# Two causal attentions: the order of score blocks, value products and turned outputs taken from a table per layer, and the row maxima of a wide row chained from its first half

## The reference, cut to what matters

```python
# layer 0: 16 heads of 8 features; layer 1: 16 heads of 64 features, keys and values made from 32 shared features
scores = jnp.einsum('bhqd,bhkd->bhqk', q, k) * scale        # B, H, S, S = 4, 16, 1024, 1024
scores = jnp.where(causal, -jnp.inf, scores)                # a query sees the keys up to its own place
attn = jax.nn.softmax(scores, axis=-1)
out = jnp.einsum('bhqk,bhkd->bhqd', attn, v)
```

## Time and profile before

| | us |
|---|---|
| median of 3 runs (2075.58 to 2084.6) | 2078.56 |
| the profiled execution | 2072.83 |
| its span | 2071.1 |
| PE busy (share of span) | 1879.1 (91%) |
| DVE busy | 1435.9 (69%) |
| ACT busy | 1193.8 (58%) |
| stretch 120 to 584, thirteen and more loaded steps of the first attention: PE, DVE busy of 464 | 450.35, 370.00 |
| stretch 1050 to 1674, thirty steps of the second attention: PE, DVE busy of 624 | 623.60, 418.01 |

### The profile page before, as it was taken

The page is one execution under the profiler, slowest core; times in us unless marked ns, Lnnn a source line. Parts: engine busy times, 40 slices in busy tenths (PEclk is TensorE's granted clock), DMA queues, the critical chain, the costliest instruction groups (busy, mean ns, idle before and its releaser), DMA issues. The chain is left out here.

```text
span 2071.1 us, 39995 instructions
## 1 busy us (share of the span) xinstructions
PE 1879.1 (91%) x9924; PEld 1169.6 (56%) x9926; DVE 1435.9 (69%) x6257; ACT 1193.8 (58%) x2252; POOL 622.0 (30%) x955
## 2 busy tenths in 40 slices
PE   5799999999986729994899999999999999899998
PEld 3455555555536527872445555555555558678886
DVE  6788777777826827875766666666666636887776
ACT  5266666666664728981445555555555558555554
POOL 4011111111120774762011111111111110567665
PEclk9799999999995869996989999999999999999999
DMA  6423233433305112224946464655555512546562
GB/s 214 123 35 64 42 61 44 61 48 55 49 8 207 36 56 70 75 76 132 362 112 145 104 139 106 136 111 130 116 126 122 119 35 81 138 93 131 128 121 61
DMA packets 107198, 210.87 MB, mean 102 GB/s; under 512 B 16540, under 2 KB 46378, under 8 KB 105680
## 3 DMA queue, kind: packets, MB, share of 16 engines
q1 hardware_dynamic: 99840, 194.98, 40.8%
q0 software_dynamic: 4992, 8.48, 1.3%
q10 hardware_dynamic: 2256, 6.21, 1.0%
HBM read 163.01 MB, written 47.89 MB: 102 GB/s over the span
## 5 line engine op out<-in xcount | busy, mean ns | idle before, releaser
L679 DVE CUSTOM_DVE_ANT_0 a1ms<-a1S,mask_q 128x128 bf16<-128x128 f32 (+1 forms) x758 | 387.9, 553 | 173.5 <-issue 170.6
L736 ACT ACTIVATE a1work<-a1T 128x512 f32<-128x512 f32 x576 | 330.2, 597 | 297.4 <-PE a1T L838 296.9
L679 DVE CUSTOM_DVE_ANT_0 a0ms<-a0S,mask_q 128x384 bf16<-128x384 f32 (+2 forms) x752 | 379.7, 553 | 97.5 <-issue 90.4
L736 ACT ACTIVATE a0work<-a0T 128x512 f32<-128x512 f32 x576 | 330.0, 597 | 186.6 <-PE a0T L838 175.7
L817 PE MATMUL a1O<-a1work,a1v 128*33 128x512 f32 (+3 forms) x1536 | 304.6, 496 | 0.9 <-POOL a1work L647 0.9
L838 PE MATMUL a0T<-a0qT,a0kT 128*128 128x512 f32 (+3 forms) x768 | 265.3, 392 | 15.9 <-ACT a0work L736 5.1
L838 PE MATMUL a1T<-a1qT,a1kT 97*128 97x512 f32 (+3 forms) x768 | 263.3, 391 | 2.0 <-DMA a1qT<-a1mr 2.0
L838 PEld LDWEIGHTS a1T<-a1qT,a1kT 97*128 97x128 f32 x768 | 131.6, 189 | 202.0 <-ACT a1work L736 144.5
L777 PE MATMUL a0S<-a0kS,a0qS 128*128 128x384 f32 (+2 forms) x752 | 229.9, 362 | 17.2 <-PEq L305 9.1
L1997 POOL TENSOR_TENSOR attn<-attn 128x512 f32<-128x512 f32 x136 | 201.4, 1496 | 105.8 <-DVE attn L1899 104.7
L838 PEld LDWEIGHTS a0T<-a0qT,a0kT 128*128 128x128 f32 x768 | 131.4, 189 | 170.2 <-ACT a0work L736 126.5
(11 more groups left out here) (336 smaller groups left out, 3333.2 us busy)
## 6 DMA issues: line engine op xcount, KB each, us to landing
attn<-scr_g SPq DMA_DIRECT2D x32, 1024.0 KB, 9.8
a1qT<-scr_q SPq DMA_DIRECT2D x93, 256.0 KB, 4.1
a1qS<-scr_q SPq DMA_DIRECT2D x90, 256.0 KB, 6.3
a1kT<-scr_k SPq DMA_DIRECT2D x93, 128.0 KB, 4.8
a1kS<-scr_k SPq DMA_DIRECT2D x90, 128.0 KB, 7.0
scr_q<-p_own SPq DMA_DIRECT2D x16, 512.0 KB, 5.1
scr_q<-attn SPq DMA_DIRECT2D x16, 512.0 KB, 7.4
scr_slots<-wp SPq DMA_DIRECT2D x1, 5980.0 KB, 18.2
```

The costliest lines, as they stand in the source:

```text
L679: nc.vector.tensor_tensor_reduce(masked_s[spare][:, 0:c1 - c0], buf[:, 0:c1 - c0], k.mask_q[:, SEQ - w + c0:SEQ - w + c1], 1.0, NEVER, ALU ...
L736: nc.scalar.activation(prob_of(g, p)[:, h, :], t_ps[slot % 2][:, :], ACT.Exp, scale=scale)\
```

## The change

A class `Order` holds, for each layer, the order of the 12 units of a head (`blocks`, now single halves), the place of the turned maxima in it (`mark`), the slot of every unit (`units`), of every value product (`values`, numbers past the last slot fall into the next step), and of the two turned output halves (`outs`). Units of one slot may now be many, and slots may have none. The lead has 6 units (before four items, also 6 units). In layer 0 the first lead unit stands in slot 31 (before 33) and the last value product in slot 2 of the next step (before 3). In layer 1 the first lead unit stands in slot 12 (before 15) and the last two value products in slot 2 of the next step (before 17 and 1), with the first product of the new step right behind them. L686 is gone: the second half of a wide row starts its maximum from the first half's result (`floor`), and waits on DVE until that is there.

```diff
+ORDER_0 = Order(((6, 0), (3, 0), (4, 0), (7, 0), (2, 0), (0, 0), (1, 0), (6, 1), (5, 0), (7, 1), (5, 1), (4, 1)),
+                5,
...
+                (9, 13, 17, 21, 25, 27, 30, 35, 38), (4, 7))
+ORDER_1 = Order(((1, 0), (4, 0), (5, 0), (6, 0), (6, 1), (4, 1), (5, 1), (2, 0), (7, 0), (7, 1), (3, 0), (0, 0)),
+                3,
+                (0, 0, 0, 0, 1, 3, 3, 3, 3, 4, 5, 6, 8, 9, 9, 10, 10, 10, 11, 12, 12, 13, 13, 15, 16, 16),
+                (2, 8, 8, 11, 11, 14, 16, 20, 20), (5, 6))
...
-    LEAD = 4
-    BLOCKS = [b for i in reversed(range(TPB // 2)) for b in (TPB // 2 + i, i)]
-    PBUF = 3 * BURST if BURST == 1 else 2 * BURST
+    LEAD, PBUF = 6, 3
...
-            NRED += 3 if i == BLOCKS[-1] and HALVES == 2 else 2
+            NRED += 2
             MAXIMA[h, i, half] = NRED
+    HEAD_DONE = [max(n for (head, _, _), n in MAXIMA.items() if head == h) for h in range(HG)]
...
+    ahead_units = [(*x, a, slot) for (x, a), slot in zip([(x, 1) for x in chain[LEAD:]] + [(x, 2) for x in chain[:LEAD]], order.units)]
+    out_units = [("o", 0, 0, half, -1, slot) for half, slot in enumerate(order.outs)]
...
     VALUES, CARRIED = ({s: [] for s in range(NSLOT)} for _ in range(2))
-    for p in range(NP):
-        for part in range(PARTS):
-            s = (p // BURST * BURST + BURST) * HG - 1 + DELAY + part * (HG // PARTS)
-            (VALUES[s] if s < NSLOT else CARRIED[s - NSLOT]).append((p, part))
+    for p, s in enumerate(order.values):
+        (VALUES[s] if s < NSLOT else CARRIED[s - NSLOT]).append(p)
...
-    COPY_0 = next(s for s in VALUES if (LAST_OF_BANK[0], PARTS - 1) in VALUES[s]) + 1
-    COPY_1 = max(s for s in CARRIED if CARRIED[s]) + 1
-    OUT_AT = COPY_1 + 2
+    COPY_AT = [order.values[p] + 1 for p in LAST_OF_BANK]
...
+                            if half:
+
+                                dve.wait_ge(red_done, lin(gU, NRED, MAXIMA[h, i, 0]))
                             dve.wait_ge(unit_ready, base + (n + 1))
                             nc.vector.memset(held[:, spare:spare + 1], 0.0).then_inc(red_done, 1)
 
                             found = mhalf[par][:, h, i - TPB // 2:i - TPB // 2 + 1] if wide and half == 0 else mmax[par][:, h, i:i + 1]
+                            floor = NEVER
+                            if half:
+                                floor = mhalf[par][:, h, i - TPB // 2:i - TPB // 2 + 1]
                             nc.vector.tensor_tensor_reduce(masked_s[spare][:, 0:c1 - c0], buf[:, 0:c1 - c0],
-                                                           k.mask_q[:, SEQ - w + c0:SEQ - w + c1], 1.0, NEVER,
+                                                           k.mask_q[:, SEQ - w + c0:SEQ - w + c1], 1.0, floor,
                                                            ALU.add, ALU.max, found).then_inc(red_done, 1)
-                            if i == BLOCKS[-1] and HALVES == 2:
-
-                                dve.wait_ge(red_done, lin(gU, NRED, MAXIMA[h, i, half] - 1))
-                                upper = mmax[par][:, h, TPB // 2:TPB]
-                                nc.vector.tensor_tensor(upper, upper, mhalf[par][:, h, :], ALU.max).then_inc(red_done, 1)
...
-                        if (h, i, half) == (0, BLOCKS[0], 0):
+                        if (kind, h, i, half) == chain[0]:
 
                             pe.wait_ge(ldS[gU[1]], gU[0] * (16 * NLOAD) + 16 * NLOAD)
...
-                        pe.wait_ge(red_done, lin(gU, NRED, MAXIMA[h, BLOCKS[-1], 0]))
+                        pe.wait_ge(red_done, lin(gU, NRED, HEAD_DONE[h]))
```

More of the change, by code:

```diff
@@ L463, in attention @@
     NLOAD = operands.NLOAD
[L464 to L467 removed]
+    LEAD, PBUF = 6, 3
+    assert 2 * NP % PBUF == 0
     DIAGONALS = [[(off, seg) for off, seg in zip((0, p[0][2] - p[0][1]), p) if seg[1] == seg[0] * P] for p in PIECES]
@@ L477, in attention @@
     for h in range(HG):
[L478 to L486, removed]
+        blocks = [("S", h, *x) for x in order.blocks]
+        chain += blocks[:order.mark] + ([("m", h - 1, 0, 0)] if h else []) + blocks[order.mark:]
+    chain.append(("m", HG - 1, 0, 0))
     MAXIMA, NRED = {}, 0
-    for kind, h, i, half, _, _ in units_from([(*x, 0) for x in chain]):
+    for kind, h, i, half in chain:
         if kind == "S":
-            NRED += 3 if i == BLOCKS[-1] and HALVES == 2 else 2
+            NRED += 2
             MAXIMA[h, i, half] = NRED
[L495 to L498, removed]
+    HEAD_DONE = [max(n for (head, _, _), n in MAXIMA.items() if head == h) for h in range(HG)]
+    start_units = [(*x, 0, 0) for x in chain] + [(*x, 1, 0) for x in chain[:LEAD]]
+    NLEAD, NU = LEAD, len(chain)
     START_MAXIMA = NRED + MAXIMA[start_units[-1][1:4]]
@@ L585, in before @@
                 return [last_of[bank] for bank in main_ring(unit_slot(g))]
-            units = units_from(own if at(g, NG - 1) else base_items)
-            return [(*x[:4], x[4] - 1, x[5]) for x in units[-BANKS:]]
+            return [(*x[:4], x[4] - 1, x[5]) for x in units_of(after(g, -1))[-BANKS:]]
         def beside(units, slot):
@@ L745, in step @@
                                     copy_max(unit_base(g), main_ring(unit_slot(g)), n, gm, hm)
-                            if slot == COPY_0:
-                                copy_out(g, 0)
-                            if slot == COPY_1 and not at(g, 0):
-                                copy_out(after(g, -1), 1)
+                            for b in range(SEQ // ST):
+                                if slot == COPY_AT[b]:
+                                    copy_out(g, b)
+                                if slot == COPY_AT[b] - NSLOT and not at(g, 0):
+                                    copy_out(after(g, -1), b)
                 main_steps(act, step)
-                copy_out(END, 1)
+                for b in range(SEQ // ST):
+                    if COPY_AT[b] >= NSLOT:
+                        copy_out(END, b)
             @block.tensor
@@ L792, in _, with values @@
                     unit(start_units, None, start_ring, n, (0, 0))
[L794 to L799 removed]
+                by_value = [(p, x) for p in sorted(range(NP), key=lambda p: order.values[p]) for x in segments[p]]
+                opens, closes = [{x[0][1] // ST: (p, x) for p, x in way} for way in (by_value[::-1], by_value)]
+                def values(g, p):
+                    if DIAGONALS[p]:
                         pe.wait_ge(masked, lin(g, PER_MASK, NDIAG[p]))
[L802 removed]
+                    else:
                         pe.wait_ge(exp_done, lin(g, NSLOT, (p + 1) * HG))
[L804 removed]
+                    if p == 0 and at(g, 0):
                         pe.wait_ge(red_done, START_MAXIMA)
@@ L809, in values @@
                             nc.tensor.matmul(o_ps[:, b * ST:(b + 1) * ST], zero[:, 0:P], zero, start=True, stop=True)
-                    if part == 0 and p < SEQ // ST and not at(g, 0):
+                    if p < SEQ // ST and not at(g, 0):
                         pe.wait_ge(o_copied, lin(g, 2, p - 1))
-                    for x in parts[p, part]:
+                    for x in segments[p]:
                         seg, off, q0, q1 = x
@@ L818, in values @@
                                                     prob_of(g, p)[:, h, off:off + q1 - q0],
-                                                    start=opens[bank] == (p, part, *x), stop=closes[bank] == (p, part, *x))
-                    if part == PARTS - 1:
-                        last.then_inc(pv_done, 1)
+                                                    start=opens[bank] == (p, x), stop=closes[bank] == (p, x))
+                    last.then_inc(pv_done, 1)
                 def step(g):
```

60 lines of the change are left out of this document (27 added, 33 removed), and 2 rows, old and new, of the table ORDER_0.

## The result

| | before | after |
|---|---|---|
| median, us | 2077.07 (2073.8 to 2084.6, 4 runs) | 2117.86 (2111.29 to 2119.73, 4 runs) |
| ratio to before | | 1.0185, 95% interval 1.015 to 1.0221 |
| profiled execution | 2072.83 | 2117.76 |
| its span | 2071.1 | 2116.0 |
| mean distance of the loads of successive steps, layer 0 | 33.5 | 32.4 |

The change made the kernel 1.9% slower, 20 us beyond the end of the forecast range. Layer 0 gained 1.0 us a step in place of 2.2. Layer 1 lost 2.2 us a step in place of 0.9.

The account below looks back on a forecast made before the run. The prediction took PE's work and waits in both attentions' main steps as the bound, with loads deciding. Terms -33, -2 and +26 make -9 on the profiled 2072.8, 2064; the median is 5.7 above, so 2069 us, range 2034 to 2098.

Parts of the forecast that it names:

- What bounds the kernel: Main steps of both attentions: PE work, plus waits and changes of work, 7.6 of 33.5 us in a layer-0 step.
- The term of the loads: Lead units' wait for loads: layer 0's loads hardly have slack, and this small wait decides the forecast.
- The slots of layer 0: Layer 0's new unit order: 30.3 us a step by the slot sum, against 33.5 measured before.
- The loads of layer 0: Layer 0's first lead unit: slow loads make two in five steps 32.7 us, 31.3 overall; term -33 us.
- L686 and the floor: DVE maxima in both layers: dropping L686 gives -2 us; the second half's new wait costs up to 40 without cover.
- The slots of layer 1: Layer 1's new order: slot sum 19.7 us a step against 20.0 for the old order.
- The loads of layer 1: Layer 1's first lead unit waits 1.9 us for loads; step 21.4 against 20.5 us, +26 us over 29 steps.
- rival C: Layer 1: products wait for POOL's masks behind the late lead unit; +19 us, 2098; sign, distance over 22; chance 0.15.
- the clock: Rival in layer 1: PE's idle time drops the clock to 1.2 GHz for half of each step, +258 us, 2327; chance 0.02.

Follow-up runs that it names:

- the nine matmuls: The kernel of the change plus nine 512-column PE matmuls, whose results are overwritten, ahead of the lead unit's wait for its loads: 2099.75 us, ratio 1.012.

## Why the prediction was wrong

**What bounds the kernel** held. The term of the loads, which I had called the one that decides, decided.

**The slots of layer 0** held: the forecast was 30.3, and undisturbed steps are 30.1 to 30.3. Waits for exponentials fell from 7.7 to 6.0 us a step, not to 5, and those for banks fell by more than assumed.

**The loads of layer 0** were half right. A lead unit that waits starts 26.4 to 27.1 after SP in six steps and 25.5 in one (26.6 forecast for slow loads), and two steps with a wait but full clock took 32.8 (32.7 forecast). But seven of twelve steps waited, not two in five. Four of the seven also lost clock. With 26.4 to 27.1 for the landing and 6.1 for the rest, those four would have taken 32.5 to 33.2 and took 34.1 to 36.0: 9 us together, 0.75 a step in the mean. The term was -33. From the steps it is -13.5 in thirteen (33.48 to 32.44). That is one execution: with the same table and order of loads in layer 0, three other kernels had 32.9, 33.0 and 32.4 a step. (In the sum of the term, thirteen steps of 2.2 us are 28.6 and not 29.5, which changes nothing.)

**L686 and the floor.** In the new order the chain is largely hidden. Its price is at least the 3 us of layer 1's steps and at most the 18 between the medians; the sum had it at nothing and the bound at 40. That a chained pair costs 0.33 us of DVE was bounded rightly by L686. What I had not seen is that the chain by itself, without the new tables, would have made the kernel slower by 1.45%.

**The slots of layer 1**: 0.3 us a step had been forecast as the gain; with loads in time it is 1.1 (20.47 to 19.35). I took the table as nearly neutral, and with its loads in time it is worth 32 us in 29 steps. It needs the early lead: with the lead units late the same table gives 20.4. My slot sum for the new order, 19.7, was 0.35 too high and the one for the old, 20.0, 0.5 too low; which waits in it are wrong was not tried.

**The loads of layer 1.** The mechanism and the place were right. The lead unit starts 13.1 after SP in the mean (13.0 forecast), waits 2.2 (1.9) and a step without loss of clock takes 21.7 (21.4). By itself that makes 1.2 x 29 = 36 us in place of 26, inside the bounds of +12 to +38. A mean distance of 22.66 was to be the sign of rival C, products that wait for masks. It isn't: those waits are 0.3 us at most after the change, 8.7 in 620. The sign couldn't tell a late mask from a slow clock. Layer 1 after the change, from 1080 to 1700:

```profile
PEld a1O L822 <- POOL a1work L649: 8.7, 28, 0.3
```

**The step that failed is the clock.** I wrote that the longest idle time, 1.25 us, had left the clock alone, and gave its fall a chance of 0.02, because I had priced it as one size: half of every step, 258 us. But 1.25 us is the longest of the main steps only. The same trace, behind layer 0, has PE idle for 1.96 us after busy microseconds at full clock:

```profile
620.44 1.82 PE L887 MATMUL o0aps<-ident,o0st 128*128 128x128 f32 x8 [1.96 <-ACT o0st L913]
```

```profile
614.00:618.40 4.40, 3.97 (x26) 1.55 (x26) 0.55 (x2) 2.33 (x5) 0.00 (x0) 1.00 0.00 0
621.40:622.40 1.00, 1.00 (x6) 1.00 (x6) 0.00 (x0) 1.00 (x6) 0.63 (x2) 0.50 0.80 303
625.40:626.40 1.00, 1.00 (x11) 1.00 (x11) 0.94 (x4) 1.00 (x5) 0.00 (x0) 1.00 0.92 383
```

So the kernel before already showed the fall, to 0.50 for some 3 us; and at 694.22 it showed a gap of 1.91 us behind which the clock stayed. The fall that came lasts some 3 us and costs 1.5 us in eighteen of 28 steps of layer 1. That is 0.94 a step, 27 us, which the nine matmuls gave back (0.98 a step). With layer 0's 9 it is 36 us of the 54 between the forecast's -9 and the +44.9 of the profiled executions. Of the rest about 10 are layer 1's wait (36 in place of 26) and about 10 the steps of layer 0 that waited, seven of twelve in place of two in five. The earlier trace rows said nothing about gaps of 2 us, and the sum itself forecast one of 1.9 in every step: the term needed a bound between zero and 258 and had none. The gaps ahead of the lead units are 1.5 to 3.1 us here; TensorE: Matmul & The Clock Gate (the Trainium skill, "Why this matters for your kernels") advises to have none over about 3 us between bursts, and by it nearly all of these would be harmless. The trace differs: in eighteen of 28 steps a gap of 1.9 to 2.6 us was enough.

Put together from the traces: up to layer 1's first loads the changed kernel is 15.1 us ahead (layer 0's steps -13.5), from there to its last loads it loses 60.8 (its 29 steps 62.2, of which about 27 are the clock, and its first step -1.4), and behind them it wins 0.9. That makes the 44.9.

## What to carry to other kernels

When a reordering brings a consumer closer to the issue of its loads, work out the time from issue to need, as the earlier trace rows allow, and move the consumer or the issue together with it; here six slot numbers took the result from 1.9% slower to 1.0% faster, and the order of two blocks of SP in layer 1 to 2.4% faster. Price a new wait of 2 us on TensorE as the wait plus a possible spell at half clock behind it, look through the whole trace, not only the main steps, for gaps of that length and the clock behind them, and fill the wait with idle matmuls to separate the two. Where an engine goes back to the head of a long loop, try the kernel with bursts of loads kept away from it; in layer 0 that gave 15 us.

## What the runs showed of the hardware

- PE idle for 1.9 to 2.6 us in a step of 21 to 23, otherwise busy: granted clock 0.50 for some 3 us afterwards in eighteen of 28 steps, none in ten. Gaps of the same length (2.2 us) are in both kinds, so the length alone does not decide. What does isn't shown. The kernel before has the same pair outside its main steps: 1.96 us idle with a fall to 0.50, 1.91 without.
- DVE idle on its way back to the head of its loop in layer 0: 1.3 to 2.5 us without loads just ahead, 4.0 to 5.9 where the six loads for the lead had been issued some 2 us ahead of it. In layer 1 the same order of loads gave no such gap.
- A maximum over 128x512 on DVE that waits for and starts from the result of the one directly ahead of it: it starts 0.27 us later and lasts 0.06 longer than one that doesn't.
